# A fused attention and mixture-of-experts layer: where the experts' low halves are made, how the slot outputs are kept and sent, and who adds the last two planes

## The reference

```
x   = layernorm(x + attention(x))      # 16 heads of 128; q, k and y RMS-normed, ALiBi bias, causal softmax
out = layernorm(x + experts(x))        # 8 experts, top 2 by router logits

# experts:
top_vals, top_idx = top_k(x @ w_router, 2);  probs = softmax(top_vals)
h_e = relu(x @ w_fc[e]) ** 2;  y_e = h_e @ w_proj[e]      # 512 x 512 each
out = probs[0] * y_first + probs[1] * y_second            # of each token's two experts
```

## Time and profile before

| | |
|---|---|
| median of three timed runs | 1544.5 us (1540.76 to 1546.12) |
| the profiled execution's own time | 1543.5 us |
| its span in the profile | 1541.7 us |
| attention stage, up to the last store of y | about 959 us |
| route stage | about 959 to 1222 us |
| slot stage on TensorE | about 1222 to 1495 us |
| end, after the last matmul | about 1495 to 1541.7 us |
| TensorE busy | 1435.4 us, 93% |
| VectorE, ScalarE, GpSimd busy | 811.8, 720.6, 427.2 us |
| HBM read, written | 149.74 MB, 82.31 MB |

### The profile page before, as it was taken

One profiled execution on the slowest core, in us unless ns is written; L12 is line 12 of the kernel. 1 busy time (PEld: TensorE's weight loads), 2 busy tenths in 40 slices (PEclk: granted clock), 3 DMA queues, 4 the chain that ended last, 5 costly groups with the idle time before them and its releaser, 6 DMA issues. The chain is left out here.

```text
span 1541.7 us, 26608 instructions
## 1 busy us (share of the span) xinstructions
PE 1435.4 (93%) x7936; PEld 1210.4 (79%) x7937; DVE 811.8 (53%) x1867; ACT 720.6 (47%) x1617; POOL 427.2 (28%) x443
## 2 busy tenths in 40 slices
PE   7999999999999999999999997799999499999960
PEld 5888888888888888888888886688888377778850
DVE  6555555555655655555555554355455344444426
ACT  5565565565555655655655664222222033333323
POOL 1221221212222222212222221332333353335851
PEclk9999999999999999999999999999999699999985
DMA  5223223232232232232232252643343456664849
GB/s 166 78 80 102 69 88 99 63 96 91 65 102 86 71 102 76 80 102 75 82 102 75 82 178 71 231 144 130 110 142 130 117 178 205 230 233 164 285 172 347
DMA packets 92844, 196.52 MB, mean 127 GB/s; under 512 B 21328, under 2 KB 22096, under 8 KB 90384
## 3 DMA queue, kind: packets, MB, share of 16 engines
q1 hardware_dynamic: 81600, 137.66, 28.3%
q0 software_dynamic: 11216, 58.52, 10.3%
HBM read 149.74 MB, written 82.31 MB: 151 GB/s over the span
## 5 line engine op out<-in xcount | busy, mean ns | idle before, releaser
L328 POOL TENSOR_TENSOR small<-small,half 128x4 f32<-128x4 f32 x193 | 194.9, 1010 | 762.5 <-DVE small L357 762.5
L445 DVE CUSTOM_DVE_ANT_0 logit<-score_ps,bias 128x128 f32<-128x128 f32 (+3 forms) x256 | 124.8, 488 | 156.7 <-PE score_ps L542 118.7
L280 ACT ACTIVATE prob<-logit,small 128x128 f32<-128x128 f32 (+3 forms) x256 | 144.2, 563 | 118.4 <-DVE small L445 114.6
L555 PEld LDWEIGHTS y_ps<-vs,prob_t 128*128 128x128 f32 x1280 | 174.8, 191 | 21.9 <-ACT prob_t L287 4.5
L555 PE MATMUL y_ps<-vs,prob_t 128*128 (+1 forms) x1280 | 185.1, 275 | 1.0 <-ACT prob_t L287 0.7
L287 ACT ACTIVATE prob_t<-prob_ps 128x128 f32<-128x128 f32 (+3 forms) x256 | 111.6, 436 | 53.2 <-PE prob_ps L548 52.2
L764 ACT ACTIVATE yt_hi<-turn_ps,subln 128x512 fp32r<-128x512 f32 x64 | 44.0, 688 | 176.5 <-PE turn_ps L1029 173.9
L548 PE MATMUL prob_ps<-ident,prob 128*128 128x128 f32 x640 | 112.8, 274 | 3.3 <-ACT prob L280 3.3
L1038 PE MATMUL out_ps<-w_hi,yt_hi 128*128 128x512 f32 x256 | 107.4, 419 | 6.6 <-DVE yt_lo L867 6.6
L499 PE MATMUL k_ps<-w_hi,x_hi 128*128 (+1 forms) x256 | 103.8, 405 | 6.1 <-DVE w_lo L396 6.1
L499 PE MATMUL v_ps<-w_hi,x_hi 128*128 (+1 forms) x256 | 106.9, 418 | 0.0
(11 more groups left out here) (184 smaller groups left out, 3307.2 us busy)
## 6 DMA issues: line engine op xcount, KB each, us to landing
slots_x<-in_zeros SPq DMA_DIRECT2D x64, 512.0 KB, 5.2
y_scratch<-x_now SPq DMA_DIRECT2D x65, 256.0 KB, 3.0
x_raw<-in_x_t SPq DMA_DIRECT2D x64, 256.0 KB, 2.9
y_raw<-y_scratch SPq DMA_DIRECT2D x15, 1024.0 KB
w_raw<-in_w_experts POOLq DMA_DIRECT2D x7, 2048.0 KB, 9.1
w_hi<-in_w_experts POOLq DMA_DIRECT2D x7, 2048.0 KB, 8.5
w_raw<-in_w_all SPq DMA_DIRECT2D x16, 768.0 KB, 7.0
y_raw<-slots_x SPq DMA_DIRECT2D x39, 256.0 KB
```

Of the source, the lines that this page charges most:

```text
L280: nc.scalar.activation(prob[:, 0:width], logit[:, 0:width], ACT.Exp, scale=-1.0, bias=least[:, h:h + 1], accum_out=row_sum[:, (i % 2) * HG ...
L328: nc.gpsimd.tensor_tensor(r, ms, half[:, :], ALU.pow).then_inc(ready, 1)
L445: nc.vector.tensor_tensor_reduce(out=logit[:, 0:width], in0=score_ps[:, 0:width], in1=bias[:, h, T - width:T], scale=1.0, scalar=3e38, op0 ...
L555: mm = nc.tensor.matmul(y_ps[:, h * D:(h + 1) * D], prob_t[:, j * P:(j + 1) * P], one(vs[:, bass.ds(now, 1), j, h * D:(h + 1) * D]), start ...
```

## The change

1. *Low halves in the attention stage.* In each of the 64 attention steps SP stores the previous low block from a spare block `ew` of `w_raw` to a DRAM tensor `experts_lo` and loads the next raw block (128x512) into `ew`. GpSimd loads the same block with a cast into a second spare block and, behind its inverse roots, subtracts. The experts' two loads are afterwards of the finished halves (`w_experts` cast into `w_hi`, `experts_lo` into `w_lo`), with no subtraction. 
2. *Order at the stage's end.* The last clear of `slots_x` grows from 9 to 15 tiles and moves behind the last iteration; `w_last` and expert 0 wait for the last low block's store.
3. *Slot outputs in 31 buffers* (4 of `yo`, 8 of `w_raw`, 19 of `kept`), never in `slots_y`. ScalarE first writes share times the token's row ("preset"), which is ready before the matmuls down; VectorE then adds the PSUM result. SP loads the next x tile and notes after the preset.
4. *GpSimd* loads an expert as soon as its place is free and scatters tiles between; empty experts are left out, for which VectorE makes a few more tables.
5. *The end.* `HB` becomes 8; TensorE adds the planes of odd tiles with two identity matmuls, VectorE those of even tiles.

```diff
-KEPT = NT
-FROM_KEPT = 24
+ALL_TILES = SPARE_TILE + E - 1
+KEPT = 19
@@ attention_phase, sync: body(it, last), each i; and after it
                     n = it * TB + i
+                    sp.wait_ge(lo_ready, n + 1)
...
+                        sp.dma_start(block_of(experts_lo, (n + its * TB - 1) % (its * TB)), ew)\
+                            .then_inc(lo_stored, 16)
+                        sp.dma_start(ew, block_of(w_experts, n)).then_inc(ew_loaded, 16)
                     (the clear of two tiles)
+            sp.wait_ge(w_ready, 3 * CT)
             with sp.Fori(0, last_it) as it:
                 body(it, False)
-            left = SPARE_TILE + 1 - its * TB * CLEARED
+            body(last_it, True)
+            left = ALL_TILES - its * TB * CLEARED
             sp.dma_start(x_slots[:, its * TB * CLEARED:, :], ...).then_inc(cleared, 16)
-            body(last_it, True)
             sp.wait_ge(y_normed, its * TB + 1)
             sp.dma_start(y_scratch[its * TB, :, :], yn[:, 0, :]).then_inc(y_stored[0], 16)
+            sp.wait_ge(lo_ready, its * TB + 1)
+            sp.dma_start(experts_lo[E - 1][:, (EB - 1) * F:EB * F], ew).then_inc(lo_stored, 16)
@@ attention_phase, gpsimd
+            def split_expert_block(n, hi):
+                pool.wait_ge(ew_loaded, n * 16 + 16)
+                pool.wait_ge(ew_cast, n * 16 + 16)
+                pool.wait_ge(lo_stored, n * 16 + 16)
+                nc.gpsimd.tensor_tensor(ew, ew, hi, ALU.subtract).then_inc(lo_ready, 1)
             for i in range(TB):
-                    rstd_y(it * TB + i + 1)
+                    pool.wait_ge(lo_ready, n + 1)
...
+                    pool.dma_start(hi, src).then_inc(ew_cast, 16)
+                    rstd_y(n + 1)
                     if not (last and i == TB - 1):
-                        rstd_kq(it * TB + i + 2)
+                        rstd_kq(n + 2)
+                    split_expert_block(n, hi)
@@ route_sync, route_gpsimd
-            sp.dma_start(w_raw[:, 0:CT, :], w_last).then_inc(wp_loaded, 16)
             load_y(1, 1); load_x(0, 0); load_x(1, 1)
+            sp.wait_ge(lo_stored, 16 * (E * (CT + FT) + 1))
+            sp.dma_start(w_raw[:, 0:CT, :], w_last).then_inc(wp_loaded, 16)
             pool.wait_ge(y_turned, NHG)
-            load_expert(0); pool.wait_ge(wp_ready, HG); load_expert(1)     # halves of expert 0
+            pool.wait_ge(lo_stored, 16 * (E * (CT + FT) + 1))
+            load_expert(pool, 0, 0)
@@ slots_sync
-                sp.wait_ge(yo_ready, k + 1)
+                sp.wait_ge(preset, k + 1)
-                if not late:
-                    sp.dma_start(rows_of(y_slot[...]), yo[:, y, :]).then_inc(yo_stored[y], 16)
                 if more(k, YB):
                     load_rows(at, y)
                     load_notes(k + YB, at, y)
...
-            spread_up_to(SLOT_TILES - 3)
-            spread_up_to(sp.value_load(end_i[0:1, E - 1:E], ...))
+            spread_up_to(sp.value_load(filled_i[0:1, 0:1], min_val=2 * NT, max_val=SLOT_TILES))
@@ slots_gpsimd
+            def spread_rows(k):
+                pool.wait_ge(yo_ready, k + 1)
+                if k >= YB:
+                    pool.wait_ge(spread[k % YB], k // YB * 16)
+                pool.indirect_dma_start(rows_d, ...notes_of[:, k, 1:2]..., output_of(k), None)
+            pool.wait_ge(projected, NT)
+            pool.wait_ge(tables_known, 3)
+            for r in range(1, E):
+                expert = pool.value_load(order_i[0:1, r:r + 1], min_val=0, max_val=E - 1)
+                pool.wait_ge(we_loaded, 32 * r)
+                if r >= 3:
+                    end = pool.value_load(end_i[0:1, r - 3:r - 2], min_val=0, max_val=SLOT_TILES)
+                    pool.wait_ge(down_done, end + 1)
+                load_expert(pool, r, expert)
+                sure = r if r >= 3 else 0
+                for k in range(done, sure):
+                    spread_rows(k)
+                done = sure
+            for k in range(done, SLOT_TILES):
+                spread_rows(k)
@@ slots_scalar, slots_vector, slots_tensor
+                act.wait_ge(g_loaded[y], q * 16 + 16)        # between rectify and round_x
+                nc.scalar.activation(out, xs[:, y, :], ACT.Copy, scale=share_of(k, 2)).then_inc(preset, 1)
-                nc.scalar.activation(yo_of(k, y, late), ye_ps[b][:, :], ACT.Copy, scale=shares[:, y, 0:1])
-                nc.vector.scalar_tensor_tensor(row, xs[:, y, :], shares[:, y, 2:3], row, ALU.mult, ALU.add)
+                nc.vector.scalar_tensor_tensor(row, ye_ps[b][:, :], share_of(k, 0), row, ALU.mult, ALU.add)
+            for t in range(1, NT, 2):
+                pe.wait_ge(halves_loaded[t % HB], 32 * (t // HB) + 32)
+                nc.tensor.matmul(sum_of(t), ident[:, :], kept[:, t, :], start=True, stop=False)
+                nc.tensor.matmul(sum_of(t), ident[:, :], upper_at(t), start=False, stop=True)
```

More of the change, by code:

```diff
@@ L726, in tile_of, with load_expert @@
             return tiles[t] if isinstance(t, int) else rows_of(tiles[bass.ds(t, 1), :, :])
+        def load_expert(pool, r, e):
+            blk = expert_block(r)
+            for w, src in ((w_hi, w_experts), (w_lo, experts_lo)):
+                rows = src[e] if isinstance(e, int) else rows_of(src[bass.ds(e, 1), :, :])
+                pool.dma_start(w[:, blk:blk + CT + FT, :].rearrange("p s f -> p (s f)"), rows).then_inc(we_loaded, 16)
         def route_sync(sp):
@@ L1276, in slots_gpsimd @@
             pool.wait_ge(end_set_up, 1)
-            for t in range(0, NT, RB):
-                end_inverse_std(t, t + RB)
+            for first, last in BATCHES:
+                end_inverse_std(first, last)
         def slots_scalar(act):
@@ L1294, in slots_scalar, with slot_step @@
             round_x(1, 2)
-            def slot_step(k, b, h, y, q, late):
+            def slot_step(k, b, h, y, q, out):
                 act.wait_ge(hid_turned, k + 1)
@@ L1318, in slots_vector, with add_output @@
             nc.vector.memset(end_half[:, :], -0.5).then_inc(end_set_up, 1)
-            def add_kept(k, y, late):
-                dve.wait_ge(gated, k + 1)
-                row = yo_of(k, y, late)
-                nc.vector.scalar_tensor_tensor(row, xs[:, y, :], shares[:, y, 2:3], row, ALU.mult, ALU.add)\
+            def add_output(k, b, row):
+                dve.wait_ge(down_done, k + 2)
+                dve.wait_ge(preset, k + 1)
+                nc.vector.scalar_tensor_tensor(row, ye_ps[b][:, :], share_of(k, 0), row, ALU.mult, ALU.add)\
                     .then_inc(yo_ready, 1)
@@ L1346, in slot_step @@
                     split_x(b, k + 3)
-                add_kept(k, y, late)
+                if more(k, 1):
+                    split_hid(1 - b, k + 2)
+                add_output(k, b, out)
             slot_steps(dve, slot_step)
@@ L1362, in slots_vector @@
             for t in range(NT):
-                row = kept[:, t, :]
-                dve.wait_ge(halves_loaded[t % HB], 32 * (t // HB) + 32)
-                nc.vector.tensor_tensor(row, row, w_raw[:, t % RAW, :], ALU.add).then_inc(rows_summed, 1)
+                if t % 2 == 0:
+                    row = kept[:, t, :]
+                    dve.wait_ge(halves_loaded[t % HB], 32 * (t // HB) + 32)
+                    nc.vector.tensor_tensor(row, row, upper_at(t), ALU.add).then_inc(rows_summed[0], 1)
                 if t >= 1:
                     bias_variance(t - 1)
-                if t % RB == 2 and t > RB:
-                    scale_mean(t - RB - 2, t - 2)
-                dve.wait_ge(rows_summed, t + 1)
-                nc.vector.bn_stats(end_stats[:, t % 2, :], row).then_inc(end_stats_done, 1)
+                for first, last in BATCHES:
+                    if t == last + 2:
+                        scale_mean(first, last)
+                dve.wait_ge(rows_summed[t % 2], t // 2 + 1)
+                nc.vector.bn_stats(end_stats[:, t % 2, :], sum_of(t)).then_inc(end_stats_done, 1)
                 dve.wait_ge(end_stats_done, t + 1)
@@ L1374, in slots_vector @@
             bias_variance(NT - 1)
-            scale_mean(NT - RB, NT)
+            for first, last in BATCHES:
+                if last + 2 >= NT:
+                    scale_mean(first, last)
         def slots_tensor(pe):
```

267 lines of the change are left out of this document (132 added, 135 removed).

## The result

The changed kernel takes 1557.2 us (median of 4 runs, 1555.2 to 1558.9) against 1544.9 (4 runs, 1540.8 to 1546.1): 1.0084 times the time of before, 95% interval 1.0061 to 1.0107. It is slower, by 12 us, where 17 us less were forecast. The profiled execution took 1555.2 us, with a span of 1553.4.

The account below looks back on a forecast made before the run. TensorE was taken as busy for 93% of the span, so gains must come from the end or its slot-stage waits. Terms summed to -16.6 us from 1543.5, giving 1526.9, stated as 1527 us, range 1515 to 1544.

Parts of the forecast that it names:

- Attention: the added work: Attention stage: the added DMAs and subtractions fit in gaps and cost nearly nothing, +1.5 us, bounds 0 and +16.
- The first rival: Attention: subtractions collide with VectorE's `w_lo`, giving 1543 or 1573 us; decides from 0.38 us per step; chance 0.12.
- The waits: Slot stage: fewer waits for x tiles, -6.4 us, bounds nothing gained or all 8.8.
- The stall at step 37: Slot stage: half of the loss in step 37 goes with the changed order, -1.5 us, bounds -4 to +2.
- work off its backlog: Slot stage's end: GpSimd scatters its backlog after the last expert is issued and has caught up at tile 35.
- The fourth rival: Slot stage keeps its waits, caused by the weights' 4 MB in one burst: +7.9, 1535 us; chance 0.14.
- the end: After the slots: first plane load sooner, -12.2 us; from there to the end 37.5 us, -2.0 us.
- The third rival: End: TensorE's adds at half clock bound it, 34 us for eight tiles, +8, 1535 us; chance 0.12.
- The join: Where attention ends: the larger, later clear makes the queue behind it slip, +3.5 us, bounds -1 and +12.
- the tables: From route to slots: VectorE makes some 13 more small tables, +0.5 us, bounds 0 and +4.
- The clear's 13 us: Attention's end: the new clear moves 3.9 MB, some 13 us at 300 GB/s, and drains near 963.
- the second rival: Where attention ends: SP's queue is held for the whole clear, +12 instead of +3.5, 1535.5 us; chance 0.17.

Follow-up runs that it names:

- e8: Changed kernel with GpSimd's scatters in pairs from the eighth on, two due with each output: 1543.2 us, 1.0004 times before.
- e3: Changed kernel with 24 slot steps in loops and 15 written out, instead of 28 and 11: 1541.7 us, 0.9994 times before.
- e1: Changed kernel with SyncE's low-half store and expert-block request at the head of its attention step: 1519.3 us, 0.9856 times before.
- e10: e6 (all plane adds on VectorE) with scatters in pairs: 1521.6 us, 0.9859 times before.
- e5: e1 with the clear of the last 15 tiles issued ahead of the last attention turn: 1543.6 us, 0.9995 times before.
- e12: Kernel before with one 4 KB DMA added on GpSimd's queue in the last attention step: 1544.0 us, 1.0005 times before.
- e14: e13 with SyncE's last low half sent in the next block's first lines: 1518.2 us, 0.9835 times before.
- e13: e1 with paired scatters, each due one output sooner to catch up at number 37: 1518.3 us, 0.9843 times before.
- e6: e1 with all 16 pairs of planes added on VectorE, none on TensorE: 1534.7 us, 0.9932 times before.
- e7: e1 with 24 slot steps in loops and 15 written out: 1531.9 us, 0.9918 times before.

## Why the prediction was wrong

**The step that failed: "Attention: the added work", +1.5, measured +21.35.** The prediction put the raw load "about 4.3 us into the step", landing "some 5 us later, when the subtraction is due". The step of the earlier trace rows is one of the last turn, the one turn in which SyncE doesn't stop at the wait for x: there it stores y 0.7 us behind `x_now`, in a looped step 4.8 us behind it. `x_now` and y's store in the kernel before, in a looped step and in that of rows 8:

```profile
403.28 0.69 DVE L361 TENSOR_TENSOR x_now<-y_ps,small 128x512 f32<-128x512 f32 x1 [1.19 <-POOL small L328]
408.12 0.35 SPq L197 DMA_DIRECT2D y_scratch<-x_now  x1
...
903.05 0.69 DVE L361 TENSOR_TENSOR x_now<-y_ps,small 128x512 f32<-128x512 f32 x1 [1.19 <-POOL small L328]
903.77 0.35 SPq L197 DMA_DIRECT2D y_scratch<-x_now  x1
```

In the changed kernel's looped step the raw load is issued 6.1 us behind `x_now` (402.24 to 408.35), and GpSimd is there 4.7 us before it lands. And the new wait's cost was looked for only in what VectorE loses to the subtraction; what stood queued behind GpSimd's wait, the inverse roots of the next step, and who waits for these, `x_now`, wasn't named. Here that wait closed a ring over three engines. The bound of +16 was too small for it. The ring alone made the change worth nothing, with the time still inside the range (e8 1543.2 us, e3 1541.7); what took the time out of the range was the stall, the second step that failed, below.

**The first rival had the place but not the mechanism.** It said attention would pay, "from 18 / 48 = 0.38 us per step"; it paid 0.36 per step over 60. But the subtractions as such cost nothing (e1), and `w_lo`, which was to stand still, took 782 ns on average after against 683 before and in e1: 4.7 us in 48 instructions, all of it in six of them, which took 0.85 to 1.78 us where 0.68 is usual. Each of the six began while GpSimd subtracted. The Trainium skill's rule on this ("SBUF — State Buffer", "Who interferes with whom"), by which two SBUF inputs on VectorE and a reading GpSimd exclude each other, fits them.

**The slot stage, two terms.** The waits: -6.4 forecast. e1, without a stall, shows the term as mis-sized and not as wrong in kind: from step 2 to step 38 it takes 230.7 us (1245.13 to 1475.85) where before took 243.9, so -13.1: the 8.8 us lost before step 37, 2.2 in it (8.67 for 6.47), and 0.06 us less in each step. The end of step 38, at full and not at half clock, gives 2.1 more (4.9 for 7.0 us). The stall at step 37, -1.5: it went, but a larger one came, +14.7, for which no term stood; that is the step that failed here. The prediction saw that GpSimd would "work off its backlog", at 1.26 us for each scatter, and read it as a gain only. In the kernel before there was no such row: its GpSimd made low halves and reloaded tiles in between. What causes the stall stays open; it begins inside the row in every trace that has it. The fourth rival (the stage keeps its waits) is refuted.

**Right:** the end, -12.2 and -2.0. Against the last matmul the first load came 9.9 us sooner (8.1 us behind it before, 1.8 ahead of it after), and the last step, at full clock, is itself 2.1 us shorter; first load to end 37.2 for 37.5 forecast. The third rival, TensorE's adds as the bound: TensorE's clock was granted at 0.50 from 1522 to 1526 and at 1.00 from 1528, and a tile's two products took 2.08 and 1.91 us at the one and 1.08 and 1.02 at the other, near the prediction's 4.2 and 2.1 for a tile, but the end had the length that the transfers give it, and the same with all adds on VectorE (e10). Their share of the change is nothing. **The join**, +3.5 and +0.5 for the tables forecast, +3.8 measured for both: right in size, wrong in its reason, so the agreement is luck. The clear's 13 us at 300 GB/s had no row behind it either: it landed 17.0 us after its issue. The clear isn't what the next block waits for (e5), so the second rival falls too, and the real reason stays open (e12, e14).

With the attention term at nothing, as in e1, the sum of the forecast is 1525.4, and 1519.3 was measured in e1, which has no stall either; what is left is the slot stage's size.

## What to carry to other kernels

Where a change hangs work on an engine's queue, draw the ring: who releases its wait, what that one is waiting for in its own queue, and what waits behind it; its length stands against the shortest step and not the mean. Take an issue time from the looped step, not from a written-out last turn with fewer waits. A backlog that is freed at once is a load of its own, and has to stand in the forecast; here it can be given out with the outputs at no loss (e13). And compare versions on one chip before you call an effect the work of an edit: e5, e6 and e7 each seemed to cost 12 us and more against e1, for a stall that all programs of their chip had.

## What was not expected of the hardware

ScalarE can stand still beside GpSimd's back-to-back scatters: in five traces 15 of them, 1.27 us apart for the most part, went with gaps of 6 to 13 us on ScalarE for which the profile names no releaser, at a DMA share of 0.62 to 0.64 over the row. In three traces of another chip a row went with no gap, at a share of 0.69 to 0.75. Scatters in pairs, mostly 3.7 us between them, went with no gap on two further chips. The section of the Trainium skill named above says that "PE and ACT never wait on anyone"; that is about ports of SBUF, and no run here shows that a port is the reason, but for this row it is no guarantee. The stall repeats: all six runs of the changed kernel took 1555.2 to 1558.9 us. What decides whether it comes, the program or the chip, isn't known.
